# q's rotary embedding: the crosswise halves copied by ScalarE and multiplied by the sine on GpSimd, in an attention and mixture-of-experts kernel

## The reference

```python
h = weight[token_ids]                          # 8 x 512 tokens, width 256
h = h + attention(layernorm(h))                # 8 heads of 128, causal
h = h + moe(layernorm(h))                      # 8 experts, 1024 chosen tokens each, gelu, 1024 wide

# in the attention, for each head (and the same for k):
q = x @ w_aq                                   # [T, 128]
even, odd = q[..., :64], q[..., 64:]
q = concat([even * cos - odd * sin, even * sin + odd * cos])
s = q @ k.T / 128, masked; p = softmax(s); o = p @ v; r = o @ w_ao
```

## Time and profile before

| | us |
|---|---|
| median of three runs | 1289.47 (1289.21 to 1291.32) |
| profiled execution, whole | 1292.28 |
| its span | 1290.4 |
| TensorE busy in the span | 1146.1 (89%) |
| VectorE busy | 913.9 (71%) |
| GpSimd busy | 743.0 (58%) |
| ScalarE busy | 609.0 (47%) |

### The profile page before, as it was taken

One profiled execution on the slowest core, in us unless ns is written; L12 is line 12 of the kernel. 1 busy time (PEld: TensorE's weight loads), 2 busy tenths in 40 slices (PEclk: granted clock), 3 DMA queues, 4 the chain that ended last, 5 costly groups with the idle time before them and its releaser, 6 DMA issues. The chain is left out here.

```text
span 1290.4 us, 21944 instructions
## 1 busy us (share of the span) xinstructions
PE 1146.1 (89%) x7255; PEld 982.8 (76%) x7255; DVE 913.9 (71%) x1980; ACT 609.0 (47%) x1306; POOL 743.0 (58%) x783
## 2 busy tenths in 40 slices
PE   3899999999999999999999988015999999999995
PEld 2688887888878878878878863004999999999994
DVE  5788888898898898998988853775555555554422
ACT  3455555545545545545555543102554554554541
POOL 3676686676776766775766630006644844844425
PEclk9999999999999999999999999556999999999997
DMA  5000100100100100100000001304423523523212
GB/s 183 1 18 1 38 30 0 37 28 0 41 24 0 41 24 0 41 24 33 28 5 33 18 1 34 106 0 133 111 37 100 129 38 99 129 37 99 34 17 33
DMA packets 42170, 57.60 MB, mean 45 GB/s; under 512 B 8896, under 2 KB 34944, under 8 KB 41984
## 3 DMA queue, kind: packets, MB, share of 16 engines
q0 software_dynamic: 13824, 21.24, 9.1%
q1 hardware_dynamic: 28288, 35.58, 8.2%
HBM read 35.71 MB, written 16.91 MB: 41 GB/s over the span
## 5 line engine op out<-in xcount | busy, mean ns | idle before, releaser
L1125 DVE TENSOR_TENSOR hT_lo<-hid,hT_hi 128x512 fp32r<-128x512 f32 x128 | 89.2, 698 | 179.1 <-ACT hT_hi L1243 166.2
L268 ACT ACTIVATE prob<-bank,row_min 128x512 f32<-128x512 f32 (+3 forms) x256 | 135.9, 531 | 112.7 <-DVE row_min L389 112.6
L199 POOL TENSOR_SCALAR prob<-prob,row_inv 128x512 f32<-128x512 f32 (+3 forms) x256 | 134.5, 536 | 68.4 <-DVE row_inv L393 66.9
L1241 ACT ACTIVATE hid<-up,b_e 128x512 f32<-128x512 f32 x128 | 88.0, 688 | 155.0 <-PE up L1308 141.7
L339 DVE TENSOR_TENSOR pT_lo<-bank,pT_hi 128x384 fp32r<-128x384 f32 (+1 forms) x192 | 114.4, 596 | 50.2 <-ACT pT_hi L248 50.1
L949 POOL DMA_INDIRECT got<-routed_rows,tokens x64 | 86.3, 1349 | 103.4 <-DVE tokens L1119 84.9
L212 POOL TENSOR_TENSOR kT_lo<-k_cos,kT_hi 128x512 fp32r<-128x512 f32 x64 | 82.4, 1288 | 78.1 <-ACT kT_hi L248 78.1
L248 ACT ACTIVATE oT_hi<-bank 128x512 fp32r<-128x512 f32 x64 | 38.3, 599 | 185.7 <-PE bank L519 175.7
L206 POOL TENSOR_TENSOR q_cos<-q_cos,q_sin 128x512 f32<-128x512 f32 x64 | 82.3, 1286 | 55.4 <-DVE q_sin L376 55.2
L969 POOL DMA_INDIRECT out<-y,tokens x64 | 103.8, 1622 | 17.3 <-issue 14.8
L389 DVE TENSOR_REDUCE row_min<-bank 128x1 f32<-128x512 f32 (+3 forms) x256 | 112.6, 481 | 0.2
(11 more groups left out here) (196 smaller groups left out, 3853.0 us busy)
## 6 DMA issues: line engine op xcount, KB each, us to landing
raw<-in_w SPq DMA_DIRECT2D x16, 1024.0 KB
emb_res<-emb SPq DMA_DIRECT2D x8, 512.0 KB, 3.7
out<-h SPq DMA_DIRECT2D x8, 512.0 KB, 3.0
routed_rows<-x SPq DMA_DIRECT2D x8, 512.0 KB
x<-in_wq SPq DMA_DIRECT2D x1, 1024.0 KB, 6.1
x<-in_wk SPq DMA_DIRECT2D x1, 1024.0 KB, 9.6
x<-in_wv SPq DMA_DIRECT2D x1, 1024.0 KB, 4.9
x<-in_wo SPq DMA_DIRECT2D x1, 1024.0 KB, 8.5
```

What stands on the lines that cost most here:

```text
L199: nc.gpsimd.tensor_scalar(pr, pr, row_inv[:, h % 2, k:k + 1], 1.0, ALU.mult, ALU.mult).then_inc(s["norm_done"], 1)
L268: nc.scalar.activation(prob[:, h % 2, col:col + w], s_ps[bk][:, pc:pc + w], ACT.Exp, bias=row_min[:, h % 2, k:k + 1], scale=-1.0, accum_ou ...
L1125: nc.vector.tensor_tensor(out, in_, hi.bitcast(F32), ALU.subtract)\
L1241: nc.scalar.activation(hid[:, t % 2, :], up_ps[t % 2][:], ACT.Gelu, bias=bias)
```

## The change

q's two sine products leave VectorE. After the cosine product (now with its own semaphore q_mul), ScalarE copies the two halves of the projection crosswise from PSUM into q_sin (`swap`, at the head of its slot, semaphore q_swap). GpSimd then multiplies q_sin by the sine table in place, waits for that result (q_sin), and makes the same add as before. TensorE's waits for q_rope become waits for q_swap. k's rotation stays as it was, under the name `turn_k`.

```diff
@@ -87,7 +87,7 @@
 
         names = """wq_in wk_in wv_in wo_in tables_in w_hi w_lo consts
             ids_in emb_in res_in stats_done aggr_done var_eps rstd_done xn_ready xt_tr xt_hi xt_lo
-            q_proj k_proj v_proj q_rope k_rope q_add k_add q_hi k_hi q_lo k_lo v_hi v_lo
+            q_proj k_proj v_proj q_mul q_swap q_sin k_rope q_add k_add q_hi k_hi q_lo k_lo v_hi v_lo
             s_done s_min exp_done inv_done norm_done t_done t_hi t_lo o_done o_hi o_lo
             out_done r_evac 
             stats2_done aggr2_done var2_eps rstd2_done apart""".split()
@@ -201,8 +201,15 @@
 
             def add(b, h, x):
                 n = b * H + h
-                cos, sin = (q_cos, q_sin) if x == "q" else (k_cos, k_sin)
-                after(pool, f"{x}_rope", n + 1)
+                if x == "q":
+                    cos, sin = q_cos, q_sin
+                    after(pool, "q_swap", n + 1)
+                    nc.gpsimd.tensor_tensor(sin[:], sin[:], rope_q[:, 1, :], ALU.mult)\
+                        .then_inc(s["q_sin"], 1)
+                    after(pool, "q_sin", n + 1)
+                else:
+                    cos, sin = k_cos, k_sin
+                    after(pool, "k_rope", n + 1)
                 nc.gpsimd.tensor_tensor(cos[:], cos[:], sin[:], ALU.add).then_inc(s[f"{x}_add"], 1)
 
             def low(b, h, x):
@@ -284,6 +291,14 @@
                 after(act, "s_done", 3 * (n - 2) + 3)
                 hi_of(out[0][:, h % 2, :], cos[:], f"{x}_hi")
 
+            def swap(b, h):
+                n = b * H + h
+                after(act, "q_mul", n + 1)
+                after(act, "q_add", n)
+                nc.scalar.activation(q_sin[0:64, :], proj_ps[0][64:128, :], ACT.Copy)
+                nc.scalar.activation(q_sin[64:128, :], proj_ps[0][0:64, :], ACT.Copy)\
+                    .then_inc(s["q_swap"], 1)
+
             def v_high(b, h, i):
                 t = V_SLOT[h][i]
                 after(act, "v_proj", 2 * TB * b + t + 1)
@@ -304,6 +319,8 @@
                 for h in slots:
                     n = b * H + h
                     live = ok(h) and h < H
+                    if live:
+                        swap(b, h)
                     if ok(h - 3):
                         after(act, "o_done", n - 3 + 1)
                         after(act, "out_done", n - 3)
@@ -365,16 +382,22 @@
                     after(dve, "xt_hi", KT * b + kt + 1)
                     low_of(xT[1][:, kt, :], proj_ps[kt][:], xT[0][:, kt, :], "xt_lo")
 
-            def rope(b, h, x):
-                n = b * H + h
-                ps, table, cos, sin = ((proj_ps[0], rope_q, q_cos, q_sin) if x == "q" else
-                                       (proj_ps[1], rope_k, k_cos, k_sin))
-                after(dve, f"{x}_proj", n + 1)
-                after(dve, f"{x}_lo", n)
-                nc.vector.tensor_tensor(cos[:], ps[:], table[:, 0, :], ALU.mult)
-                nc.vector.tensor_tensor(sin[0:64, :], ps[64:128, :], table[0:64, 1, :], ALU.mult)
-                nc.vector.tensor_tensor(sin[64:128, :], ps[0:64, :], table[64:128, 1, :], ALU.mult)\
-                    .then_inc(s[f"{x}_rope"], 1)
+            def mul_q(b, h):
+                n = b * H + h
+                after(dve, "q_proj", n + 1)
+                after(dve, "q_lo", n)
+                nc.vector.tensor_tensor(q_cos[:], proj_ps[0][:], rope_q[:, 0, :], ALU.mult)\
+                    .then_inc(s["q_mul"], 1)
+
+            def turn_k(b, h):
+                n = b * H + h
+                ps = proj_ps[1]
+                after(dve, "k_proj", n + 1)
+                after(dve, "k_lo", n)
+                nc.vector.tensor_tensor(k_cos[:], ps[:], rope_k[:, 0, :], ALU.mult)
+                nc.vector.tensor_tensor(k_sin[0:64, :], ps[64:128, :], rope_k[0:64, 1, :], ALU.mult)
+                nc.vector.tensor_tensor(k_sin[64:128, :], ps[0:64, :], rope_k[64:128, 1, :], ALU.mult)\
+                    .then_inc(s["k_rope"], 1)
 
             def t_low(b, h, f):
                 n = b * H + h
@@ -454,12 +477,12 @@
                     n = b * H + h
                     live = ok(h) and h < H
                     if live:
-                        rope(b, h, "q")
+                        mul_q(b, h)
                     if ok(h - 2):
                         after(dve, "exp_done", TB * (n - 2) + 4)
                         inverse(b, h - 2, 3, 4)
                     if live:
-                        rope(b, h, "k")
+                        turn_k(b, h)
                     if isinstance(b, int) and b == 0 and h == 0:
                         after(dve, "w_hi", 7)
                         low_of(w_o[1][:], wraw_o, w_o[0][:], "w_lo")
@@ -523,7 +546,7 @@
             def xt(b):
                 after(pe, "xn_ready", b + 1)
                 for kt in range(KT):
-                    after(pe, "k_rope" if kt else "q_rope", b * H)
+                    after(pe, "k_rope" if kt else "q_swap", b * H)
                     for tb in range(TB):
                         last = nc.tensor.transpose(proj_ps[kt][:, tb * P:(tb + 1) * P],
                                                    xn[:, tb, kt * P:(kt + 1) * P], ident[:])
@@ -548,7 +571,7 @@
             def values(b, h, i):
                 n = b * H + h
                 g, jb = divmod(V_SLOT[h][i], TB)
-                after(pe, "k_rope" if i else "q_rope", n + 1)
+                after(pe, "k_rope" if i else "q_swap", n + 1)
                 products(proj_ps[i][:], [([t[:, kt, jb * P:(jb + 1) * P] for t in xT],
                                           [w[:, kt, g * 512:(g + 1) * 512] for w in w_qkv["v"]])
                                          for kt in range(KT)]).then_inc(s["v_proj"], 1)
```

## The result

The kernel after takes 1346.36 us (median of four executions, 1343.76 to 1347.5) against 1290.39 (1289.21 to 1291.88, four executions) for the kernel before: a ratio of 1.0429, 95% interval 1.0412 to 1.0446, or 56.0 us. The forecast was 1337 in a range of 1312 to 1350. The profiled execution took 1343.76 (span 1342.0), 51.5 above that of before.

The account below looks back on a forecast made before the run. Two nearly touching limits: TensorE and the q_cos-to-q_cos loop. Six middle batches add 36.6 us, first and last about 5.5 each, together + 48: profiled 1292.28 becomes 1340, or 1337.5 on the timed scale; range 1312 to 1350.

Parts of the forecast that it names:

- The mechanism: Loop from one head's q_cos to the next: GpSimd's multiply lengthens the path to q_hi, so the loop overtakes TensorE; 1337 us.
- Rival (b): Same loop at about half the price, heads 5 and 6 partly covered by TensorE's work: 1313 or 1306 us; chance 0.11.
- Rival (c): VectorE's queue time is what counts, so relieving it makes the kernel faster: 1280 us; chance 0.07.
- The path: From q_cos on VectorE to q_hi on ScalarE: grows by 1.12 us, from 3.55 to 4.67.
- The self-wait: GpSimd, between q's new multiply and the add: waits for its own result, priced at 0.08 us.
- the 0.30 of VectorE's relief given back: Heads 3, 4 and 7: t_low of fill 0 no longer waits behind oT_lo, taking 0.30 us off the growth.
- The two heads in which the multiply comes wholly on top: Heads 5 and 6, where GpSimd's rsqrt or gather ends later than the copies: + 1.37 us each.
- head 0 where it is covered: Head 0, two value blocks: its 11.84 us pass ends waiting for TensorE and hides the growth, + 0.
- The six middle batches: Attention stage: + 6.1 us a batch summed over the heads, 36.6 us for the six.
- rival (d): GpSimd's chain collides with gathers and layernorm, or TensorE's clock falls: 1 to 2 us more a batch, 1350 to 1355; chance 0.06.
- TensorE's waits: For v_lo from 1.1 us to several per batch, for xT_lo rising, for k_sin near zero.
- The picture of one loop: From one q_cos to the next through q_hi: a pass of 10.42 us, against TensorE's 10.94 for an ordinary head.

Follow-up runs that it names:

- e2: Kernel after without GpSimd's sine multiply and the wait for its result, both copies kept: 1286.42 us, ratio 0.9983 to the kernel before.
- e3: Kernel before with one more sine multiply of q and a self-wait on GpSimd, VectorE keeping all its products: 1352.20 us, ratio 1.0483.
- e6: Kernel after with q_hi moved to right ahead of k's high part on ScalarE, and k's add ahead of q's low part on GpSimd: 1277.95 us.
- e1: Kernel before with k's two sine multiplies left out on VectorE in all heads but the first: 1288.44 us, ratio 0.9986.
- e9: Kernel after, unchanged, profiled once more: 1343.58 us in one execution.
- e5: Kernel before with q_hi moved to right ahead of k's high part on ScalarE, and k's add ahead of q's low part on GpSimd: 1307.48 us.
- e7: Kernel before with q_hi moved between t_high of fill 0 and exp 0 in ScalarE's queue: 1290.98 us, ratio 1.0001.
- e8: Kernel after with q_hi moved between t_high of fill 0 and exp 0 in ScalarE's queue: 1321.61 us, ratio 1.0242 to the kernel before.
- e11: Kernel before with q_hi between t_high of fill 0 and exp 0, and k's add ahead of q's low part on GpSimd: 1278.47 us, ratio 0.9907.
- e12: Kernel after with the two copies straight instead of crosswise, halves not swapped: 1346.77 us in one execution.

## Why the prediction was right, and where it was off

**The mechanism held.** The price is GpSimd's multiply in the path from q_cos to q_hi: taking it out restores the time (e2), adding it alone brings the loss (e3), and moving q_hi behind what it held up makes it free (e6). Rival (b), that heads 5 and 6 hide the multiply, fell with q_hi at 6.11 and 5.89 there, 1.36 and 1.38 later than before. Rival (c), that VectorE's queue time is what counts, fell with e1 and e3: relief without the longer path gives 2 us, and in e3 the loss comes although VectorE keeps all its work. Both hold for the order of the queues as it was.

**The terms.** The path grew by 1.18 instead of 1.12: the copies take 1.20 from the first start to the second's end, not 1.07, because they start 0.61 apart; the multiply then starts at + 1.97, not + 1.90. In head 4, as in 3 and 7, only the copies hold it, which the prediction did not list. The self-wait is 0.08 (540.79 - 539.43 - 1.28), as priced. With the 0.30 of VectorE's relief given back, an ordinary pass grows by 0.88 (predicted 0.82). One reading of the prediction is off without effect: from q_hi at 554.03 to the end of v_lo at 558.25 is 4.22 us, not 4.26.

Pass by pass, heads 0 to 7, from the q_cos starts of one batch: predicted 11.84, 11.24, 12.41, 11.53, 11.24, 13.39, 14.84, 11.75; measured 11.88, 11.32, 12.49, 11.62, 11.31, 13.38, 14.85, 11.88. The two heads in which the multiply comes wholly on top, and head 0 where it is covered, came out within 0.04. The others are 0.07 to 0.13 longer, mostly by the copies. Sum 98.73 against 98.24 predicted: 0.5 us in each of six batches, 3 us.

**What the sum lacked.** The six middle batches took 43.0 us more (4 x 6.63 + 8.4 + 8.1) against 36.6: 3.2 of the difference are passes longer than predicted, mostly by the copies, and about 3.2 are the clock at two head 0s (e9, without the first of these falls, has 0.2 us of its 1.8 left). That is the mild form of rival (d); I priced it at 1 to 2 us in every batch and it came in two of six. The first batch cost 4.2 and the last 5.9 where I had 5.5 each. The router and experts, taken as unchanged, took 1.4 less.

From 1340 for the profiled execution to the 1343.76 measured it is so 3.2 + 3.2 - 1.3 + 0.4 - 1.4, or 4.1; the 0.3 too much is rounding in the sum. The median lies another 2.6 above the profiled execution, while that of before lay 1.9 below its own. The three other executions have a granted clock of 0.953 or 0.954 against 0.955, so clock falls are the likely cause; no trace of those executions shows it.

**Signs.** Right: VectorE - 88.8, GpSimd + 80.4 (82 forecast), q_hi at 4.73 after q_cos (6.11 and 5.89 in heads 5 and 6), batches of 98.8, no wait for k_sin. Off: ScalarE's + 72.8 (60 to 70), by the same copies, 0.59 each. Wrong: TensorE's waits. I expected most of them at v_lo and xT_lo; v_lo has 4.9 us, xT_lo did not rise (4.7 after 5.4), and 26.8 stand at exp 0. I followed the loop from q_hi to v_lo and overlooked that the last scores, ahead of the next head in TensorE's queue, wait for exp 0's bank. The lateness is the same; it is paid one station earlier.

**The picture of one loop was too simple.** It sufficed for this change, since this lengthened the leg that was longest or level. It failed when I used it to improve the kernel: q_hi late in the kernel before was to gain and cost 17 us (e5), and q_hi in the middle gained nothing or stayed 31 us above (e7, e8), because of VectorE's own leg and GpSimd's, which e5 and e8 show, and because of the stretched normalisations in head 5 (e7). Most of e5's 17 us are the 0.52 us in series: heads 3, 4 and 7 are longer by just that, head 2 by 0.3, head 6 by 0.44. Head 5 is 12.07 after 12.02, so the stretch there only takes back what the move gave.

## What to carry to other kernels

Before moving work off a queue that looks full, find which step it stands in front of: here 88 us less on VectorE cost 56, since the replacement added 1.37 us to a path on which ScalarE's whole in-order queue waited. Compare every leg of the loop from one head to the next, for the second longest decides what a repair is worth. When a path is late, see first what is queued behind it, and on which leg its new place lies: changing the place of two instructions took 12 us off the kernel before (e11) and 68 us off the kernel after (e6), while VectorE's relief alone had given 2. A place two steps further down the queue cost the kernel before 17 us (e5).

## What the hardware showed beside this

Two copies of 64x512 fp32 from one PSUM bank into one tile take 0.59 us each and start 0.60 to 0.61 apart, crossed or straight (e12); the 128x512 pair of the earlier trace rows took 1.07 for both, from two banks into two tiles. Whether the common bank, the common tile or the half partitions do this was not tried.

VectorE's fp32 operation from SBUF to SBUF went from 0.34 to 1.35 us beside a busy GpSimd (e5), while oT_lo, which reads PSUM, kept its 0.69 beside GpSimd's add.

TensorE's pauses of 1.15 and 0.78 us stood ahead of a granted clock of 0.50 in the kernel after (610.70). Ahead of the head 0 of 115.25 it had paused 1.22 and 0.79 us, and the clock fell; in e9, the same kernel, it paused 1.23 and 0.79 at that place and the clock stayed at 1.00. So the pauses alone do not decide it, and what does is not shown.
